# A graph network's second pass: each tile's window product takes its own 64 one-hot columns instead of 128

## The reference

```
h   = relu(bn(concat(x[src], edge_attr) @ W1 + b1))      # per edge, bn over all edges
s   = segment_sum(h, dst);  agg = s / max(count, 1)      # per node
h2  = relu(bn(concat(x, agg) @ W2 + b2))                 # per node, bn over all nodes
out = layernorm(x + relu(h2 @ Wl + bl))
```

## Time and profile before

| | us |
|---|---|
| median of three runs | 587.01 |
| profiled execution | 587.13 |
| its span | 585.4 |
| first pass and the constants, to the first product of line 925 | 449.8 |
| second pass, first product to the last copy of line 1162 | about 96.7 |
| after it | about 39 |

### The profile page before, as it was taken

How to read it: one execution, slowest core, us unless ns; L and a number is a source line. 1 busy time by engine, 2 the same in 40 slices (tenths; PEclk the granted TensorE clock), 3 DMA queues, 4 the chain that set the end, 5 groups by cost and what they waited for, 6 DMA issues and landing times.

```text
span 585.4 us, 10554 instructions
## 1 busy us (share of the span) xinstructions
PE 526.8 (90%) x3117; PEld 463.1 (79%) x3117; DVE 508.8 (87%) x719; ACT 421.7 (72%) x850; POOL 363.2 (62%) x464
## 2 busy tenths in 40 slices
PE   4679999999999999999999988888998999999993
PEld 4557878877777878888888877776877999999683
DVE  5796999999999999999999999998976877777787
ACT  3458877787778877888888887777767655655476
POOL 4776777777777777777777777777770333333500
PEclk9779999999999999999999999999999999999997
DMA  7744554445544555444444444444345789886004
GB/s 201 253 157 141 170 173 150 143 158 176 171 157 141 170 175 164 150 154 154 147 151 150 144 154 157 157 133 143 108 141 180 269 273 300 288 283 181 2 1 111
DMA packets 48140, 97.02 MB, mean 166 GB/s; under 512 B 10886, under 2 KB 23605, under 8 KB 48100
## 3 DMA queue, kind: packets, MB, share of 16 engines
q1 hardware_dynamic: 30734, 63.38, 32.7%
q0 software_dynamic: 10912, 22.37, 13.8%
q10 hardware_dynamic: 6453, 10.79, 5.0%
HBM read 70.11 MB, written 26.37 MB: 165 GB/s over the span
## 4 chain that ended last, share of the span: by engine, by line
PE 58%; DVE 13%; POOL 8%; issue 7%; DMA 7%; ACT 6%; ACTq 0%; DVEq 0%; POOLq 0%
PE psT L783 26%; PE psH L925 7%; PE psC L925 6%; POOL res L681 6%; PE psH L765 5%; PE psT L846 4%; DMA res<-ytab,srci 3%; PE psC L765 3%; DVE node_hot L1320 2%; ACT node_hot L1096 2%; DVE psX L1335 2%; PE psH L792 1%; ACT node_rows_turned L1086 1%; ACT node_hot L1099 1%; PE psT L838 1%
## 5 line engine op out<-in xcount | busy, mean ns | idle before, releaser
L681 POOL DMA_INDIRECT res<-ytab,srci x265 | 250.1, 944 | 81.8 <-issue 75.9
L783 PE MATMUL psT<-node_hot,node_table 125*128 125x384 f32 x1250 | 260.7, 357 | 5.1 <-DVE node_hot L1320 4.6
L783 PEld LDWEIGHTS psT<-node_hot,node_table 125*128 125x128 f32 x1250 | 220.8, 190 | 30.0 <-issue 12.8
L1320 DVE TENSOR_TENSOR node_hot<-agg,psC 125x1920 fp32r<-125x1920 int32 x75 | 160.9, 2147 | 0.0
L1096 ACT ACTIVATE node_hot<-agg,nodeid 125x384 fp32r<-125x384 int32 x250 | 131.7, 603 | 6.6 <-PE psT L783 4.5
L1099 ACT ACTIVATE node_hot<-node_hot,ones 125x1920 fp32r<-125x1920 f32 x50 | 95.1, 1902 | 1.6
L1436 DVE TENSOR_TENSOR work<-res,psX 128x512 f32<-128x512 f32 x104 | 70.7, 687 | 21.8 <-PE psH L925 11.7
L706 POOL TENSOR_TENSOR agg<-agg,srci 128x64 f32 x104 | 32.0, 308 | 76.6 <-ACT srci L1162 73.8
L765 PE MATMUL psH<-w1e,work 128*128 128x256 f32 x268 | 70.5, 385 | 6.8 <-DVE work L1305 3.0
L681 POOL DMA_INDIRECT work<-ytab,srci x64 | 62.1, 970 | 21.7 <-issue 17.1
L1335 DVE TENSOR_TENSOR psX<-agg,psX 128x512 f32<-128x512 f32 x103 | 71.1, 690 | 4.5 <-ACT agg L1033 4.5
(11 more groups left out here) (222 smaller groups left out, 536.4 us busy)
## 6 DMA issues: line engine op xcount, KB each, us to landing
work<-in_edge_attr SPq DMA_DIRECT2D x26, 512.0 KB, 3.4
res<-spill SPq DMA_DIRECT2D x25, 512.0 KB, 4.2
spill<-work SPq DMA_DIRECT2D x13, 512.0 KB, 2.7
spill<-res SPq DMA_DIRECT2D x12, 512.0 KB, 2.7
agg<-in_src_rows SPq DMA_DIRECT2D x25, 192.0 KB, 3.9
res<-ytab,srci POOLq DMA_INDIRECT x265, 2.5
hot_dram<-hotb ACTq DMA_DIRECT2D x13, 256.0 KB, 3.1
hot_dram<-work ACTq DMA_DIRECT2D x13, 256.0 KB, 3.1
```

What stands on the lines that cost most here:

```text
L681: pool.indirect_dma_start(rows[:, j * F:(j + 1) * F], None, ytab, bass.IndirectOffsetOnAxis(ap=srci[:, j, g:g + 1], axis=0)).then_inc(gath ...
L783: last = pe.matmul(rows_at, table[0:PN, part, (t0 + t) * F:(t0 + t + 1) * F], hot_now[0:PN, t, :], start=(n == 0 and t == 0 and part == 0) ...
L1320: dve.tensor_tensor(dve_hot(i, d)[0:PN, :, :], rows[i % 2][0:PN, :].bitcast(I32).unsqueeze(1).broadcast_to([PN, CUT, HOTW]), nodep[:, t0:t ...
```

## The change

Three of the four products of a group lose the 64 columns that nobody reads: 64 moving columns instead of 128. The fourth is as it was. The number, the order and the waits of all instructions stay as they were, on every engine; the constant BEYOND goes.

```diff
-BEYOND = 64
...
                 for j in range(TILES):
-
-
-                    n = min(WIN + BEYOND, (TILES - j) * WIN)
-                    last = pe.matmul(psA[q][:, 0:n], mx[:, q, j * F:(j + 1) * F], hotf[:, q, j * WIN:j * WIN + n],
+                    last = pe.matmul(psA[q][:, 0:WIN], mx[:, q, j * F:(j + 1) * F], hotf[:, q, j * WIN:(j + 1) * WIN],
                                      start=(j == 0), stop=(j == TILES - 1))
                 last.then_inc(summed, 1)
```

## The result

The changed kernel takes 670.14 us (median of four runs, 668.03 to 671.69) against 587.44 us before (four runs, 585.83 to 587.97): 1.140 times as long, interval 1.137 to 1.144. Slower, as forecast, and the median 3 us above the 667 us. Its profiled execution took 671.69 us with a span of 669.9, 84.5 more than before.

What follows compares the result with a forecast made beforehand. TensorE's products of line 925 were taken to bound the second pass, at 0.1116 us a record. The sum was 587.1 + 80.7 - 3.2 + 2 = 666.6, rounded to 667 us; range 585.3 to 676.

Steps and rivals of the forecast that it cites:

- The load sets a record at full clock: Second pass: loading the stationary 128 x 128 sets 0.112 us a record, so fewer columns save 0 at full clock.
- rival 3: Second pass: narrow records' loads run closer than 0.112 us, VectorE then bounds the group; 16 us less, 571 us; chance 4%.
- The clock falls at the thin stretch: TensorE, little busy at 446.84 to 449.75 us just before the second pass: the clock falls to 1.2 GHz about there.
- these 3.2: Start of the second pass: first four groups at full speed before the clock falls, -3.2 us.
- Rival 1: Second pass: the clock holds and the load hides everything, 587 us (585.5 to 588.8); chance 36%.
- A fallen clock stays low through the pass: Second pass: 64-column records stream half the time at 1.2 GHz too, so nothing raises the clock.
- 0.213 us a slow record: Second pass at 1.2 GHz: a record takes 0.213 us, the streaming of 128 columns at that clock.
- The 0.195 us by the length of the load's record: Second pass: alternative slow-record price, from load records lasting 336 ns at 1.2 GHz against 192, 1.75 times as long.
- +80.7 for the pass: Second pass: 832 records at 0.213 us make 177.2 us instead of 96.5, its pauses vanishing.
- +2 for the node products: Node products behind the second pass: they begin slow until the clock rises, losing 1.4 to 2.8 us, say +2.
- Rival 2: Second pass: the clock swings or falls late; 627 us with half slow, anything from 590 to 647; chance 12%.

Runs made afterwards that it cites:

- run 1: Changed kernel with 128 columns in the first three of 26 steps, 64 in the other 23: 588.12, 589.64, 599.20 and 654.23 us.
- experiment 2: Changed kernel, 64 columns throughout, with the thin stretch before the pass filled with unread products: 586.90, 589.18, 652.09 and 665.56 us.
- run 3: Changed kernel with 128 columns in steps 9 to 11, 64 in all others: 615.57, 616.17, 617.23, 619.23 and 648.79 us.
- run 6: Kernel before with 112 columns instead of 128 for the first three tiles: twelve runs from 585.17 to 589.48 us, ratio 1.000.
- run 7: Changed kernel with only the first 32 columns of each 64-column window, the rest left out of the sums: 668.11 and 668.81 us, 1.138 times before.
- run 4: 96 columns for the first three tiles in every step, against 64 in the changed kernel: seven runs 586.23 to 589.29 us, others 635.62, 670.53 and 671.40.
- run 9: Kernel of experiment 2 plus two useless VectorE operations between steps 0 and 1, so TensorE pauses: 671.66 to 672.93 us, ratio 1.142.
- run 10: Kernel before (128 columns), thin stretch filled, plus two useless VectorE operations between steps 0 and 1: 592.15 to 592.81 us, ratio 1.007.
- run 5: Kernel before (128 columns) without its unread products ahead of the pass: nine runs 587.32 to 590.51 us, ratio 1.0023, and a tenth of 1053.31.

## Why the prediction was right, point by point

**The load sets a record at full clock: right, shown.** Runs 1 to 3 have 64-column streams at 2.4 GHz with 1.79 us for 16 records. Less than 128 columns gain nothing, so rival 3 (faster) has nothing left. By the formula of the Trainium skill ("TensorE: Matmul & The Clock Gate", Back-to-back issue gap) a group should have taken little over half as long; the runs side with the earlier trace rows. The same section of the Trainium skill gives that formula for an isolated product and says that in a stream of loads and products both of them set the spacing; read so, it agrees with the 0.112 us. That it is the load and not some fixed cost of a record, one record of the kernel before bears out, at full clock, with one stationary column and 104 moving ones:

```profile
15.71 0.09 PEld L737 LDWEIGHTS psT<-ident,res 104*1 104x1 f32 x1
15.80 0.30 PEld L751 LDWEIGHTS psH<-w1x,res 128*125 128x125 f32 x2
```

The next load starts 0.09 us behind it, not 0.112, and 104 columns at 0.84 ns are 0.087 us. It is a single record, though the other profiles have it too.

**The clock falls at the thin stretch: right in place, off in time, and in part luck.** I let it fall after four groups and took off 3.2 us for these; in the profiled execution it had fallen 0.05 us before the first product. The sum was made for the profiled execution, and there it is 5.1 us short of 671.69: these 3.2, 1.0 for the later start, 0.6 for the pass and 0.2 behind it. My reason for a fall was that narrow products follow the thin stretch. In this execution it fell before any of them had run, and TensorE's gaps ahead of the pass, 0.94 and 0.98 us, are those of the kernel before, whose profile kept the clock.

Seven profiled executions have this thin stretch: in four it fell, from 0.05 us before the first product to 2.7 behind it (after and run 3 with 64 columns, run 6 with 112, run 7 with 32), in three it held (before and run 1 with 128, run 4 with 96). So the narrow products are not needed for the fall, but why all eleven executions that began the pass with 64 or 32 columns there came out slow, and only three of the ten with 96, is open. Rival 1 speaks of the one fall that the rows show, but they hold two: the clock was also full to 32.78 us and low from 37.06, and between these TensorE was idle for 3.92 us.

**A fallen clock stays low through the pass: right, shown** by run 3 (it rises with the wide products and not before) and the pair of runs 9 and 10. This was the choice on which the forecast stood; no row of before showed it. That a fall in the kernel before heals is right too, but not at once: with 112 or 128 columns the rise came 3.3 to 5.7 us behind the first wide product (runs 3, 5, 6 and 10).

**0.213 us a slow record: right**, measured 3.41 / 16 = 0.2133. It was a guess from an equality at full clock. That the columns do not make it, run 7 shows, as half of them change nothing; that the load does is the best account, not shown. The 0.195 us by the length of the load's record would have been 15 us short.

**+80.7 for the pass and +2 for the node products**: 81.3 and 2.2, the clock rising 5.0 us behind the first node product (630.10 to 635.05). The 1.0 us by which the pass began later was not in the sum.

**Rival 1 (the clock holds)** was the right account of a kernel whose thin stretch and pauses spare it, as in two runs of experiment 2, and the wrong one here. **Rival 2 (a late or passing fall)** did not occur in the four runs of the changed kernel; the times and mean clocks of single executions of runs 1 to 4 (599 to 666 us) fit it, none of them profiled.

## What to carry to other kernels

Columns of a moving operand that nobody reads are not always waste: where something else sets the pace, here the load of the stationary operand, they cost no time, and they can be what lets TensorE's clock come back. Before narrowing a product, look at the granted clock around every pause of that stage, and ask what the slow stream would look like: if it is as thin at 1.2 GHz as at 2.4, one pause of 4.4 us can make a whole stage nearly twice as slow. Time such a change in several executions: with 96 columns one kernel gave 587 and 671 us.

## What the runs showed of the hardware that was not expected

- Two stable speeds of one instruction stream: with 64 columns steps at 3.41 us and at 1.79 us for 16 records stand in one execution (run 3).
- Products with a 128 x 128 load in f32 stand 0.112 us a record apart at 2.4 GHz and 0.213 at 1.2, with 32 columns as with 64; the load's record lasts 192 and 333 ns.
- At a full clock the narrow stream outlived short pauses: in run 3 the 7.3 us from 532 us on hold 6.24 us of work and kept 2.4 GHz. In run 9, with 1.59 us of work in 5.80, the clock fell.
